# Moving the second half's recurrence behind the start of the experts, with waits on exactly what is read and new orders and banks

## What is computed

```
x = x + tanh(g_xattn[0]) * wkv(w, u, k=layernorm(x), v=ctx)        # a recurrence over the 256 tokens
x = x + tanh(g_ffn[0])   * qffn(layernorm(x), w_gate, w_up, w_down)# ternary weights, tokens as integers
x = x + tanh(g_xattn[1]) * attention(layernorm(x), ctx)            # 32 heads of 8, normed q and k
x = x + tanh(g_ffn[1])   * moe(layernorm(x))                       # 64 experts, top 8, and a shared one

# wkv, one step t for every batch and channel
no = max(o, u + k[t]);  A = exp(o - no);  E = exp(u + k[t] - no)
y[t] = (A*p + E*v[t]) / (A*q + E)
no2 = max(w + o, k[t]); A2 = exp(w + o - no2); E2 = exp(k[t] - no2)
p, q, o = A2*p + E2*v[t], A2*q + E2, no2
```

## Time and profile before

| | |
|---|---|
| time, median of 3 runs (lowest, highest) | 478.23 us (477.91, 479.02) |
| span of the profiled execution | 476.0 us |
| TensorE busy (matmul), share | 399.1 us, 84% |
| VectorE busy, share | 375.6 us, 79% |
| ScalarE busy, share | 301.7 us, 63% |
| granted TensorE clock, mean | 0.956 |
| DMA | 47.47 MB, mean 100 GB/s |

### The profile page before, as it was taken

How to read it: one execution, slowest core, us unless ns; L and a number is a source line. 1 busy time by engine, 2 the same in 40 slices (tenths; PEclk the granted TensorE clock), 3 DMA queues, 4 the chain that set the end, 5 groups by cost and what they waited for, 6 DMA issues and landing times.

```text
span 476.0 us, 7786 instructions
## 1 busy us (share of the span) xinstructions
PE 399.1 (84%) x2612; PEld 191.0 (40%) x2612; DVE 375.6 (79%) x801; ACT 301.7 (63%) x442; POOL 0.2 (0%) x4
## 2 busy tenths in 40 slices
PE   1041866677786999999999999999999999999996
PEld 1010344333334445544434333554444444444443
DVE  5999599999998989999986975895456677777754
ACT  5888686689795865678976677463234444444422
POOL 0000000000000000000000000000000000000000
PEclk9995699689898899999999999999999999999999
DMA  8520000000003360383433233244413556653101
GB/s 294 227 67 0 1 1 1 1 1 0 2 2 101 121 211 24 93 232 117 138 104 109 89 110 109 83 143 149 145 67 134 170 168 170 169 172 130 67 22 44
DMA packets 31506, 47.47 MB, mean 100 GB/s; under 512 B 5610, under 2 KB 15210, under 8 KB 30956
## 3 DMA queue, kind: packets, MB, share of 16 engines
q1 hardware_dynamic: 31468, 46.98, 31.6%
HBM read 45.65 MB, written 1.31 MB: 99 GB/s over the span
## 4 chain that ended last, share of the span: by engine, by line
PE 60%; DVE 21%; ACT 9%; issue 5%; DMA 2%; SPq 2%; DVEq 0%; ACTq 0%
PE ps L1622 32%; PE ps L1956 16%; PE ps L1731 4%; PE ps L1719 2%; DVE bn L1044 1%; ACT regO L608 1%; SPq L563 1%; DVE xn L1063 1%; PE ps L1741 1%; DMA regC<-in_ctxT_dram 1%; PE ps L1647 1%; ACT regW L629 1%; PE ps L1613 1%; DVE regO L1272 1%; DVE kc L1178 1%
## 5 line engine op out<-in xcount | busy, mean ns | idle before, releaser
L1529 DVE TENSOR_TENSOR regW<-ps,regW 128x512 f32<-128x512 f32 x64 | 44.1, 690 | 53.8 <-PE ps L1622 51.2
L1622 PE MATMUL ps<-hH,regC 128*128 128x512 f16 x264 | 85.5, 379 | 0.0
L959 ACT ACTIVATE regW<-ps 128x512 f32<-128x512 f32 x51 | 30.4, 596 | 85.0 <-PE ps L1622 82.0
L1622 PE MATMUL ps<-hH,regW 128*128 128x512 f16 x248 | 81.5, 384 | 1.1 <-DVE regW L1529 1.1
L1622 PE MATMUL ps<-hL,regC 128*128 128x512 f16 x132 | 50.0, 379 | 0.0
L1956 PE MATMUL ps<-regW,regC 128*128 128x512 f16 x198 | 48.2, 379 | 0.0
L1622 PE MATMUL ps<-hL,regW 128*128 128x512 f16 x124 | 47.5, 383 | 0.0
L1512 DVE TENSOR_TENSOR regW<-regW 128x512 f16<-128x512 f32 x64 | 43.6, 682 | 0.7 <-ACT regW L972 0.5
L1956 PE MATMUL ps<-regW 128*128 128x512 f16 x180 | 43.8, 379 | 0.2 <-DVE regW L1512 0.2
L972 ACT CAST regW<-regW 128x512 f16<-128x512 f32 x64 | 39.2, 613 | 2.0 <-DVE regW L1550 1.8
L1622 PEld LDWEIGHTS ps<-hH,regC 128*128 128x128 f16 x264 | 25.8, 98 | 31.6 <-issue 2.3
(11 more groups left out here) (210 smaller groups left out, 692.2 us busy)
## 6 DMA issues: line engine op xcount, KB each, us to landing
regW<-routing_dram SPq DMA_DIRECT2D x130, 128.0 KB, 3.0
fw<-in_gu_dram SPq DMA_DIRECT2D x31, 256.0 KB, 3.1
regP<-in_gu_dram SPq DMA_DIRECT2D x25, 256.0 KB, 3.1
fw<-in_dp_dram SPq DMA_DIRECT2D x31, 128.0 KB, 3.1
regP<-in_dp_dram SPq DMA_DIRECT2D x25, 128.0 KB, 3.1
regO<-in_ffn_dram SPq DMA_DIRECT2D x3, 1024.0 KB, 9.2
x<-in_x_dram SPq DMA_DIRECT2D x2, 512.0 KB, 8.2
regC<-in_ctxT_dram SPq DMA_DIRECT2D x1, 1024.0 KB, 5.2
```

Source lines behind the costliest of these rows:

```text
L959: nc.scalar.activation(sgm[:, c % 2, :], bank(gate_bank(c)), ACT.Silu, scale=UNSCALE).then_inc(esilu_done, 1)
L1529: V.tensor_tensor(rows, bank(gate_bank(c) + 1), rows, ALU.mult).then_inc(et_done, 1)
L1622: mm = T.matmul(out_ap, w(k), a(k), start=(n == 0), stop=(n == 3 * DK - 1))
```

## The change

The change rewrites the orders of all five engines. What it does, part by part:

- The second half's recurrence gets buffers of its own (in regO, regF and exs; `halves`), its values are loaded a second time into accS by SP (`load_values_again`), and its steps go to other places: `running_max(2)` at the end of the list ahead of chunk 0, `clamps`, `sums` and `quotient` beside chunks 0 to 4, `turn_y(1)` beside chunk 5, the norm, token scales and FFN of the second half beside chunks 5 to 14, its attention beside 15 to 27, its last norms beside 27 and 28, logits beside 30, routing beside 30 and 31.
- The first nine weight entries are split ahead of chunk 0 (five before).
- VectorE's steps become generators: `post` notes by name what an instruction writes, `after` waits for named ones, and `run(name, ..., steps=n)` issues n instructions of a step, so that two chains can be interleaved. There is a place "P" between the gated and the plain product of a tanh chunk.
- Root chains get buffers by norm and by rows (`norm_set`, `rows_set`), the hidden scales and reciprocals of heads two sets.
- `BY_TANH` is 0 and 17 to 27 (11 to 22 and 26 before); ScalarE changes its tables more often beside chunks 0 and 2. `LOAD_IN` is a written table. The two-buffer stage of weight loads holds to entry 25 (`MORE`).

The diff, cut to its core:

```diff
+        wk1 = {n: cut(regO, 1024 * i, 1024).rearrange("p (b n) -> p b n", b=2) for i, n in enumerate(names)}
+        halves.append((wk1, O1, Pn1, Qn1, kT1, YN1, accS))
...
-        MORE = 11
+        MORE = 26
...
         BESIDE_SCALAR = {
+            (0, "A"): [("exponentials", 2, 0), ("turned_weights", 0, 4), ("exponentials", 2, 1), ("table_silu",)],
+            (2, "A"): [("table_exp_ln",), ("reciprocal_guess", 2)],
+            (2, "B"): [("table_silu",)],
+            (3, "B"): [("weights_high", 9), ("weights_high", 10)],
...
+            (30, "B"): [("table_exp_tanh",), ("exp_logits", 1), ("table_silu",)],
+            (31, "B"): [("turned_weights", 1, 4)],
...
         BESIDE_VECTOR = {
+            (0, "P"): [(("weigh", 0), 2)],
+            (0, "A"): [(("weigh", 0), None), (("clamps", 2), None), (("sums", 2), 6)],
+            (1, "A"): [(("sums", 2), 1)],
+            (1, "B"): [(("sums", 2), 2)],
+            (2, "A"): [(("sums", 2), None)],
+            (2, "C"): [(("quotient", 2), 1)],
+            (3, "C"): [(("weights_low", 9), None), (("quotient", 2), 1)],
+            (4, "C"): [(("quotient", 2), None), (("weights_low", 10), None)],
+            (5, "A"): [(("add_y", 1, 4), None)],
+            (5, "B"): [(("stats", 7), 6)],
...
+            (15, "C"): [(("stats", 9), None), (("rows", 5), 1), (("norm", 9), 1), (("rows", 5), 1),
...
+            (28, "A"): [(("norm", 11), 1), (("norm", 10), 1), (("norm", 11), 1), (("norm", 10), 1),
...
+            (30, "C"): [(("weigh", 1), 1), (("logits", 1, 4), None), (("weigh", 1), None)],
...
         BESIDE_PRODUCTS = {
+            (1, "A"): [("turn_weights", 0, 4)],
+            (5, "B"): [("turn_y", 1, 4)],
+            (10, "B"): [("turn_norm", 7, 4)],
+            (11, "A"): [("wide_products", 4, 0, 4), ("wide_products", 4, 1, 6)],
...
+            (29, "B"): [("turn_norm", 10, 4), ("turn_norm", 11, 5)],
+            (30, "A"): [("logits", 1, 4)],
+            (31, "B"): [("turn_weights", 1, 4)],
...
-        BY_TANH = tuple(range(11, 23)) + (26,)
+        BY_TANH = (0, 17, 18, 19, 20, 21, 22, 23, 24, 25, 26, 27,)
...
+            def load_values_again():
+                sp.wait_ge(y_ready, 2)
+                sp.dma_start(accS[:, :, :], ctxT_in[:, :, HALF:NT]).then_inc(ld_late, 16)
...
-            def settle():
-                dve.wait_ge(v_ord, done[0])
-            def link(ins):
-                post(ins)
-                settle()
+            def post(ins, *what):
                 done[0] += 1
+                for w in what:
+                    stands[w] = done[0]
                 ins.then_inc(v_ord, 1)
+            def after(*what):
+                dve.wait_ge(v_ord, max(stands[w] for w in what))
...
+            def run(name, *at, steps=None):
+                if (name, at) not in begun:
+                    begun[name, at] = begin(name, at)
+                left = steps
+                while left != 0 and next(begun[name, at], "ended") != "ended":
+                    left = None if left is None else left - 1
```

The end of VectorE's new list ahead of chunk 0, and of TensorE's:

```diff
+            run("norm", 6, steps=6)
+            run("low_halves", 5, 0)
+            run("norm", 6)
+            run("logits", 0, 1, steps=9)
+            run("running_max", 2, steps=4)
+            run("logits", 0, 1)
+            run("running_max", 2)
...
+            turn_norm(5, 0)
             logits(0, 1)
+            turn_norm(6, 2)
```

More of the change, by code:

```diff
@@ new lines, in _ @@
+            run("quotient", 0)
+            run("weight_scales", steps=1)
+            run("quotient", 1)
+            run("low_part", 1)
+            run("low_part", 2)
+            run("add_y", 0, 0)
+            run("stats", 1)
+            run("weight_scales")
+            run("norm", 1, steps=1)
+            run("ternary_weights", 0)
+            run("norm", 1)
+            run("rows", 0, steps=1)
+            run("token_scales", 0, steps=1)
+            run("rows", 0, steps=1)
+            run("token_scales", 0, steps=1)
@@ new lines, in _ @@
+            run("heads_out", 0, 2)
+            run("heads_sum", 9, 6)
+            run("heads_sum", 10, 7)
+            run("heads_out", 1, 6, steps=2)
+            run("heads_sum", 11, 2)
+            run("heads_out", 1, 6)
+            run("stats", 4, steps=3)
+            run("heads_sum", 12, 3)
+            run("stats", 4)
+            run("norm", 4, steps=1)
+            run("heads_sum", 13, 2)
+            run("norm", 4)
+            run("heads_sum", 14, 2)
+            run("low_halves", 4, 3)
@@ new lines, in _ @@
+            run("running_max", 2, steps=3)
+            run("heads_sum", 15, 2)
+            run("split_low", 8)
+            run("split_low", 9)
+            run("heads_out", 2, 0)
+            run("heads_out", 3, 2)
+            run("stats", 5, steps=3)
+            run("stats", 6, steps=1)
+            run("stats", 5)
+            run("stats", 6, steps=1)
+            run("norm", 5, steps=1)
+            run("stats", 6, steps=2)
+            run("norm", 5, steps=1)
+            run("stats", 6, steps=2)
@@ new lines, in _ @@
+            run("norm", 5, steps=1)
+            run("stats", 6)
+            run("norm", 5, steps=1)
+            run("norm", 6, steps=1)
+            run("norm", 5, steps=1)
+            run("norm", 6, steps=1)
+            run("norm", 5)
+            run("norm", 6, steps=6)
[5 more added lines that the diff above has]
+            run("running_max", 2)
+            def beside(c, place):
+                for (name, *at), n in BESIDE_VECTOR.get((c, place), ()):
+                    run(name, *at, steps=n)
@@ L1567, in _ @@
                 if c < NCH:
+                    if c in BY_TANH:
+                        experts_gated(c)
+                        beside(c, "P")
                     experts_product(c)
```

1579 lines of the change are left out of this document (882 added, 697 removed).

## The result

The changed kernel takes 473.65 us (median of 4 runs, 472.30 to 474.76) where the kernel before takes 478.07: a ratio of 0.9908, 95% interval 0.9891 to 0.9926, 4.4 us less. Its profiled execution spans 471.3 us, 4.7 less than the 476.0 before. The forecast was 476.0: the right side, and half the size.

What follows compares the result with a forecast made beforehand. Bound by VectorE and, in the attention, ScalarE up to chunk 0, then by TensorE's work and pauses: 476.0 - 4.9 + 2.7 = 473.8, plus 2.2 around the span gives 476.0 us; range 465 to 483.

Steps and rivals of the forecast that it cites:

- step 3: Chunks 6 to 33: TensorE pauses 4.0 us after 1.3, so 2.7 us lost; bounds 1 and 9.
- Step 1: Prologue: without the second half's recurrence chunk 0 starts at 137.2 us, 17.2 earlier; bounds 131 and 145.
- Step 2: Chunks 0 to 5: 13.6 us of TensorE pauses and 18.2 us of deferred work leave 4.9 of 17.2 us.
- my own sign (under 9): Chunks 0 to 5: the forecast counts as wrong if the pauses are under 9 or over 19 us.
- Step 4: VectorE's waits on the instruction just before: 0.10 us each, some 60 places, 4 to 6 us, already inside the walks.
- Rival (d): VectorE: interleaving saves nothing, the 0.10 us being the pipe's and not the wait's; 480 us, chance 0.08.
- Rival (b): TensorE's clock stays at the 1.2 GHz level through chunks 3 to 5; with late second routing 481 to 483 us, chance 0.18.
- Rival (a): Shorter prologue, chunk 0 at 133 us, and pauses of 10 us instead of 13.6; 468.2 us, chance 0.30.

Runs made afterwards that it cites:

- e2_load1: The changed kernel with one more VectorE pass over 512 elements, into a tile nobody reads, in each of chunks 7 to 30; 479.73 us, ratio 1.0027.

## Why the prediction was half right

The direction held, and so did the form of the account, a gain ahead of chunk 0 most of which chunks 0 to 5 give back. So did most ends: chunk 0 within its bounds, TensorE's losses in chunks 0 to 5 too, no pause over 2 us at the second routing, the clock back at full from chunk 3. The size did not: 2.2 us less were forecast, 4.4 were measured, and the reason lies in step 3 with what steps 3 and 4 made of the exact waits. By its steps:

Step 1, the prologue. The first exponential at 87.1 for 86, the stretch 37.0 for 37.5. The tail took 15.8 for the 13.7 walked, just inside its bound of 16: the turns of norm 5 wait 4.25 us, the clock falls, and logits, turns and all behind them run at half of it. The runs with the empty matmuls show just this, 13.7 us. 14.5 us gained for 17.2. What was wrong is the reason I gave: in the attention stretch I let the recurrence's own ScalarE time account for 8.4 of 14.3 us, where it is 5.1 of 14.8, so that this stretch came out right is in part luck. Out of the kernel before it is worth 5.1 us; the other 9, by subtraction, are the order's, and they hang on the exact waits, for with full waits ahead of chunk 0 it starts 8.3 us later (148.2 for 139.9). They are no net gain: with the small recurrence in both kernels, in(6) less the deferred work is level.

Step 2, chunks 0 to 5. 34.4 us for 35.7, 12.3 lost for 13.6, 17.9 us of deferred work for 18.2. But I had all of the loss as pauses behind VectorE. 5.6 us are pauses, which by the letter of my own sign (under 9) is a miss; the other 6.7 are TensorE's busy time over its 22.1 us of work, most of it the half clock, which I had priced only as a bound and a rival. It costs nothing here, since VectorE would not have been ready (34.7 us at a clock of 0.95, 34.4 at 0.78). The size held because VectorE sets the pace, whatever fills TensorE's time; the cause that I gave for it, VectorE's work with the recurrence in it, was only half of it. y was no longer waited for (turn_y at 32.0, walked 33.4). And the walk had the routing rows at 15.6 and the sums' end at 16.6 side by side without drawing the conclusion: each covers the other. Taking out the one gives nothing, the other 2.4 us, both 7.8. The term was 1.3 too high. Of 4.9 us that were to be left at in(6), 3.9 were, tail and chunks together.

Step 3, chunks 6 to 33, is the step that failed. I took 4.0 us of pauses after 1.3 and so 2.7 lost; TensorE paused 0.1 us up to 338.0 and 5.2 in all behind in(6), 0.7 less than before. The term was off by 3.4 us, with its sign, and that is the miss: a span of 473.8 forecast and 471.3 measured, 3.4 from here less the 1.0 that in(6) came short of. The places were right, as e2_load1 shows for three of the four; VectorE's load was not: 131.6 of 163.8 us, 80%, where I had summed 138 of 159, 87%. At 88% the kernel pauses 2.7 us there and runs 5.1 us longer behind in(6), against the 2.7 us that I took. I had counted "less 4 for chains that are interleaved" in that load, and then still put pauses at the norms. With full waits beside the chunks the same order loses 8.7 us behind in(6), with 5.2 us of pauses at just the norms and the routing that I had named (1.9 at norms 8 and 9 for my 2, 1.7 at norms 10 and 11 for my 1.6, 1.6 at the routing for my 0.4 to 2). So the pauses that I forecast are about those that this order has with full waits; the exact waits, and the interleaving that they allow, take them away.

Step 4, exact waits. The 0.10 us read from the earlier trace rows was near (0.12 to 0.16 measured). Wrong was the count: 4 to 6 us "inside the walks already", where the waits in the new order are worth 17. I had priced only the waits saved where VectorE was last. Rival (d), that interleaving saves nothing, is refuted at four times the price I gave it.

Rival (b), the clock held down through chunks 3 to 5, didn't come: from 161 to 175 us it is at 0.98. The order of events was as feared (0.50 from 131 to 144 and from 152 to 161), but it ended with the first unbroken down and gate products. Rival (a) gave 468.2 by a shorter prologue and smaller pauses; neither came, the 2.4 us under my forecast came from behind chunk 6.

## What to carry to other kernels

A move pays by what already lies idle at its new place: here VectorE would have waited 5 us for the routing rows in chunk 0 (the trace with the small recurrence shows the wait), and the recurrence fills that time. Look for the wait that nobody names because a queue hides it, and when you walk a list, ask of two ends that fall together what happens if either goes.

Exact waits and interleaved chains go together: the order gains only what the waits let it (8.3 us ahead of chunk 0 and 9.5 behind it here), and where each step needs the one before an exact wait names the same instruction as a full one. A kernel with exact waits in the old order was not run. Price them over the whole kernel, not only where the engine is last.

When work is put later, ask what reads its output next and also what its reading frees: an entry used in chunk 9 frees the staging tile that a load, and everything behind that load on its queue, waits for (by the trace of the version that lost 14 us).

## What the hardware did that I had not expected

The same instructions take different times in the prologue from run to run. The first 28 widening products of the feed-forward layer, in the changed kernel and in the one with early routing rows, which has the same matmuls up to there:

```profile
49.42 7.61 PE L1943 MATMUL ps<-fw,regF 128*128 128x512 bf16 x28 [1.36 <-ACT regF L747]
```
```profile
48.86 8.85 PE L1947 MATMUL ps<-fw,regF 128*128 128x512 bf16 x28 [1.36 <-ACT regF L751]
```

The granted clock was 0.50 up to 51 us in both; it was 0.68 over the next 2 us and then 1.00 in the one, and 0.50 and 0.69 in the other, which had it at 1.00 from 55. Chunk 0 came at 139.9 in the one and 141.9 in the other. A change that saves 2 us in such a stretch can't be read from one profile.

TensorE's waits were priced wrongly in both directions by its clock. In the tail of the prologue, where its matmuls are on the chain, half clock cost 1.9 us (15.6 us for 13.7); in chunks 0 to 5, where TensorE was busy 28.8 us at a clock of 0.78 and 24.8 us at 0.95, nothing.
